# A mixture whose router runs two tiles ahead, with one wide masked product and bias matmuls of 128 rows

## What is computed

```python
h = layernorm(x).reshape(T, 256)                             # T = 2048 tokens
logits = (h @ router_w.T + router_b).reshape(T, O, E)        # O = 256, E = 8
probs = softmax(logits, axis=-1)
w, sel = top_k(probs, 2)
w = w / sum(w, axis=-1, keepdims=True)
c = zeros((T, E)).at[t_idx, sel].add(w)                      # summed over the 256 channels
expert_out = einsum('th,eoh->teo', h, expert_w) + expert_b
x = x + einsum('te,teo->to', c, expert_out)
```

## Time and profile before

| | us |
|---|---|
| median of 3 runs (1390.74 to 1395.88) | 1393.72 |
| the profiled execution | 1396.64 |
| its span | 1394.9 |
| VectorE busy | 1010.1 (72%) |
| TensorE busy | 1107.3 (79%) |
| the mixture, 347 to 718 | 371.0 |

### The profile page before, as it was taken

How to read it: one execution, slowest core, us unless ns; L and a number is a source line. 1 busy time by engine, 2 the same in 40 slices (tenths; PEclk the granted TensorE clock), 3 DMA queues, 4 the chain that set the end, 5 groups by cost and what they waited for, 6 DMA issues and landing times. The chain is left out here.

```text
span 1394.9 us, 19404 instructions
## 1 busy us (share of the span) xinstructions
PE 1107.3 (79%) x6516; PEld 586.0 (42%) x6576; DVE 1010.1 (72%) x1854; ACT 453.5 (33%) x708; POOL 355.1 (25%) x353
## 2 busy tenths in 40 slices
PE   0687878886576979779849788788796789999996
PEld 0243434443333434334313336354372645556564
DVE  7479696874379898999875763946939278777775
ACT  1044343432243242432403331413412034444442
POOL 7024151424224342343430120210203052000000
PEclk9699999998788988899969999999997899999998
DMA  2412112110000100101000000000000010000001
GB/s 90 120 50 60 62 51 72 46 32 4 35 0 0 39 1 0 38 0 38 0 16 1 8 24 1 16 16 0 23 8 15 16 41 6 1 1 0 0 1 61
DMA packets 36263, 34.66 MB, mean 25 GB/s; under 512 B 8024, under 2 KB 32856, under 8 KB 36192
## 3 DMA queue, kind: packets, MB, share of 16 engines
q1 hardware_dynamic: 36192, 33.75, 8.2%
HBM read 27.28 MB, written 6.29 MB: 24 GB/s over the span
## 5 line engine op out<-in xcount | busy, mean ns | idle before, releaser
L926 POOL TENSOR_TENSOR wt<-lg,mid 128x2048 f32<-128x2048 f32 x16 | 75.4, 4710 | 188.4 <-DVE mid L1118 188.4
L750 DVE TENSOR_REDUCE bm<-ps 128x4 f32<-128x512 f32 x160 | 104.5, 671 | 16.6 <-PE ps L547 15.3
L672 ACT ACTIVATE pt<-ps 128x1024 f32<-128x1024 f32 (+1 forms) x96 | 83.0, 881 | 98.6 <-PE ps L593 97.2
L543 PE MATMUL ps<-ks,qs 96*128 96x512 bf16 (+3 forms) x256 | 71.1, 324 | 44.5 <-DVE bm L750 28.1
L1040 ACT ACTIVATE wt<-wt 128x2048 f32<-128x2048 f32 x16 | 30.6, 1914 | 193.9 <-POOL wt L926 193.9
L487 POOL TENSOR_SCALAR_AFFINE_SELECT pt<-pt 128x256 f32<-128x256 f32 (+1 forms) x96 | 46.8, 491 | 154.3 <-ACT pt L672 154.3
L1753 DVE SCALAR_TENSOR_TENSOR g<-g,ps 128x512 f32<-128x512 f32 x64 | 43.9, 686 | 54.2 <-ACT g L1703 54.0
L1497 DVE TENSOR_TENSOR qk_lo<-ps,qk_hi 128x512 bf16<-128x512 f32 x80 | 54.8, 685 | 38.5 <-ACT qk_hi L1399 38.3
L1399 ACT ACTIVATE qk_hi<-ps 128x512 bf16<-128x512 f32 x80 | 47.8, 597 | 102.7 <-PE ps L1290 102.7
L1290 PE MATMUL ps<-xT_hi,wq_hi 128*128 128x512 bf16 x150 | 60.5, 404 | 22.9 <-DVE qk_lo L1497 20.8
L1290 PE MATMUL ps<-wp_hi,oT_hi 128*128 128x256 bf16 x256 | 72.2, 282 | 7.9 <-DVE oT_lo L1489 7.9
(11 more groups left out here) (220 smaller groups left out, 3030.8 us busy)
## 6 DMA issues: line engine op xcount, KB each, us to landing
qs<-scratch_q SPq DMA_DIRECT2D x64, 64.0 KB, 2.6
ks<-scratch_k SPq DMA_DIRECT2D x64, 64.0 KB, 2.6
q_next<-in_w_qkv SPq DMA_DIRECT2D x4, 768.0 KB, 4.5
X<-in_x SPq DMA_DIRECT2D x4, 512.0 KB, 7.0
w_next<-in_router_w SPq DMA_DIRECT2D x4, 512.0 KB, 4.1
w_next<-in_expert_w SPq DMA_DIRECT2D x4, 512.0 KB, 5.0
p_next<-in_w_proj SPq DMA_DIRECT2D x4, 512.0 KB, 5.5
out<-X SPq DMA_DIRECT2D x4, 512.0 KB, 4.9
```

The costliest lines, as they stand in the source:

```text
L543: pe.matmul(ps[:, o + P * i:o + P * (i + w)], qs[0:SHIFT, h, P * j:P * (j + 1)], ks[0:SHIFT, h, P * k0:P * (k0 + w)], start=(i == 0), stop ...
L672: act.activation(pt[kt][:, heads[0]:heads[-1] + 1, :], src, ACT.Exp).then_inc(s_exp, 1)
L750: ins = dve.tensor_reduce(bm[:, 2 * g + i // 5, 4 * (i % 5):4 * (i % 5) + 4], src.rearrange("p (k q) -> p k q", k=4), AX_X, ALU.max)
L926: pool.tensor_tensor(wt[:, :, :], lg[t % 2][:, :, :], over_experts(mid), ALU.subtract).then_inc(s_mid, 1)
```

## The change

The program's other parts stay but for GpSimd's first instructions.

- `tiles` also yields the tile two ahead. TensorE makes `router(n+2)` where it made `router(n+1)`; `router(1)` now stands before the first pass. At t=2 `x_transposed` and `experts(n)` now come before `router(n+2)`. ScalarE makes `logits(n+2)` before `sigmoids(n+1)`, and at t=2 behind `x_parts`.
- `masked`, one product over 128x2048 written into `far`, takes the place of the eight products on VectorE; ScalarE sums its eight parts into `cw` with eight copies (`token_weights`). GpSimd's `from_middle` waits for the product (`kept`), `from_second` for the sums before it overwrites `far`.
- `statistics`, `rstd_ops` and `normalised` of the next batch come one pass earlier, at t=0 and t=1.
- `ones4` and `stage` are 128 rows, all but the first four of them zeros; GpSimd clears both.

```diff
             @block.gpsimd
             def _(pool):
+                pool.memset(glob["stage"][:, :, :], 0.0).then_inc(rows_set, 1)
+                pool.wait_ge(rows_set, 1)
                 for e in range(E):
                     pool.memset(glob["stage"][0:4, 0, D * e:D * (e + 1)], -e * ZERO_STEP).then_inc(rows_set, 1)
-                pool.memset(glob["stage"][0:4, 1, :], 0.0).then_inc(rows_set, 1)
...
         rw_hi, rw_lo, ew_hi, ew_lo = (glob[n] for n in ("rw_hi", "rw_lo", "ew_hi", "ew_lo"))
-        b3 = glob["stage"][0:4, :, :]
+        b3 = glob["stage"]
...
         wp_q = [w[:, :, :].rearrange("p (q h) n -> p q h n", q=B) for w in (glob["wp_hi"], glob["wp_lo"])]
-        ones4 = st.sb("ones4", [4, P], BF16)
+        ones4 = st.sb("ones4", [P, P], BF16)
...
         s_mid, s_far, s_wt, s_cw = st.sem("from_middle"), st.sem("from_second"), st.sem("sigmoids"), st.sem("token_weights")
-        s_c, s_u = st.sem("summed"), st.sem("experts")
+        s_kept, s_c, s_u = st.sem("kept"), st.sem("summed"), st.sem("experts")
         s_abs, s_pert = st.sem("magnitudes"), st.sem("ties_broken")
...
         def tiles(b, last):
+            def later(t):
+                return (b, t) if t < 4 else None if last else (b + 1, t - 4)
             for t in range(4):
-                yield t, 4 * b + t, ((b, t + 1) if t < 3 else None if last else (b + 1, 0))
+                yield t, 4 * b + t, later(t + 1), later(t + 2)
         with nc.Block() as block:
...
                 pool.memset(half[:, :], -0.5).then_inc(const, 1)
-                pool.memset(ones4[:, :], 1.0).then_inc(const, 1)
+                pool.memset(ones4[:, :], 0.0).then_inc(const, 1)
+                pool.wait_ge(const, 2)
+                pool.memset(ones4[0:4, :], 1.0).then_inc(const, 1)
...
                     wait_alone(pool, s_top, TOP * n + TOP, passed_pool)
                     if not isinstance(n, int) or n:
-                        wait_alone(pool, s_cw, E * n, passed_pool)
+                        wait_alone(pool, s_kept, n, passed_pool)
                     pool.tensor_tensor(wt[:, :, :], lg[t % 2][:, :, :], over_experts(mid), ALU.subtract).then_inc(s_mid, 1)
                 rstd_ops(pool, mv, rstd, half, s_mv, s_rstd, 0, passed_pool)
...
                 from_middle(0, 0)
                 def batch(b, first, last):
-                    for t, n, after in tiles(b, last):
-                        if t == 1 and not last:
+                    for t, n, after, _ in tiles(b, last):
+                        if t == 0 and not last:
...
             @block.tensor
             def _(pe):
-                pe.wait_ge(const, 2 + E)
+                pe.wait_ge(const, 3 + E)
                 def products(out, x_hi, x_lo, w_hi, w_lo, cols, bias):
                     pe.matmul(out, ones4[:, :], bias, start=True, stop=False)
...
                 x_transposed(0)
                 router(0, 0, 0)
+                router(0, 1, 1)
                 def batch(b, first, last):
-                    for t, n, after in tiles(b, last):
-                        if after:
-                            router(after[0], n + 1, after[1])
+                    for t, n, _, routed in tiles(b, last):
                         if t == 2 and not last:
                             x_transposed(b + 1)
-                        experts(n, t)
+                            experts(n, t)
+                            router(routed[0], n + 2, routed[1])
+                        else:
+                            if routed:
+                                router(routed[0], n + 2, routed[1])
+                            experts(n, t)
                 all_batches(pe, batch)
...
                 def x_parts(b):
                     reach(act, s_xblo, 4 * b)
+                    reach(act, s_rt, NU * 4 * b)
...
                     act.wait_ge(s_mid, n + 1)
                     act.activation(wt[:, :, :], wt[:, :, :], ACT.Sigmoid, scale=2.0).then_inc(s_wt, 1)
+                def token_weights(n, t):
+                    act.wait_ge(s_kept, n + 1)
+                    for e in range(E):
+                        act.activation(far[:, e, :], far[:, e, :], ACT.Copy, accum_out=cw[t % 2][:, e:e + 1]
+                                       ).then_inc(s_cw, 1)
...
                 sigmoids(0)
+                logits(1, 1)
+                token_weights(0, 0)
                 def batch(b, first, last):
-                    for t, n, after in tiles(b, last):
+                    for t, n, after, routed in tiles(b, last):
                         if after:
                             tile_high(after[0], n + 1, after[1])
-                            logits(n + 1, after[1])
                         if t == 2 and not last:
                             x_parts(b + 1)
+                        if routed:
+                            logits(n + 2, routed[1])
                         if after:
                             sigmoids(n + 1)
+                            token_weights(n + 1, after[1])
                         if t == 0:
                             act.wait_ge(load_next, 32 * b + 32)
...
                 def from_second(n, t):
+                    reach(dve, s_cw, E * n)
                     dve.tensor_tensor(far[:, :, :], lg[t % 2][:, :, :], over_experts(m2), ALU.subtract).then_inc(s_far, 1)
-                def token_weights(n, t):
+                def masked(n):
                     dve.wait_ge(s_far, n + 1)
                     dve.wait_ge(s_wt, n + 1)
-                    for e in range(E):
-                        dve.scalar_tensor_tensor(wt[:, e, :], far[:, e, :], 0.0, wt[:, e, :], ALU.is_ge, ALU.mult,
-                                                 accum_out=cw[t % 2][:, e:e + 1]).then_inc(s_cw, 1)
+                    dve.scalar_tensor_tensor(far[:, :, :], far[:, :, :], 0.0, wt[:, :, :], ALU.is_ge, ALU.mult
+                                             ).then_inc(s_kept, 1)
                 def weigh(b, n, t):
                     c_t = cw[t % 2]
...
                 from_second(0, 0)
-                token_weights(0, 0)
+                masked(0)
                 def batch(b, first, last):
-                    for t, n, after in tiles(b, last):
+                    for t, n, after, _ in tiles(b, last):
+                        if t == 0 and not last:
+                            statistics(b + 1)
                         if t == 1 and not last:
-                            statistics(b + 1)
-                        if t == 2 and not last:
...
                             from_second(n + 1, after[1])
-                            token_weights(n + 1, after[1])
+                            masked(n + 1)
```

## The result

The changed kernel takes 1401.14 us in the median (1400.03 to 1404.95), the kernel before 1393.72 (1390.74 to 1395.88): ratio 1.0058, 95% interval 1.0037 to 1.008. Both medians are of five runs. It is half a per cent slower. The profiled execution took 1400.52 us.

What follows compares the result with a forecast made beforehand. VectorE's order of work was taken to set the pace, with a second chain through ScalarE and TensorE nearly as long. Mixture +5.6, clock +1.3 and starts +0.9 made +7.8 us on 1393.72, so 1401.5; range +2 to +13.

Steps and rivals of the forecast that it cites:

- The rounds: Mixture, from one two_greatest start to the next, t = n mod 4: 19.1, 20.6, 28.9, 20.8 us for t=0 to 3.
- The last batch: Last batch of the mixture: t=0 and t=1 carry no preparation, 18.8 and 20.6 us against 20.75 and 20.5, so -1.9.
- The second chain: ScalarE's and TensorE's work from one wide product's end: sums, |logits|, ties, experts, then weigh, far, product; 17.5 us a round.
- Tail: End of the mixture: sums now stand between the last product and weigh(15), 3.0 - 0.6 + 0.1 = +2.5 us.
- The sums: ScalarE's eight accumulating copies of 128x256: 0.38 us each, 3.0 together, bounds 2.4 and 4.8.
- The bank gaps: TensorE: 0.2 us a bank around the four-row bias matmul, taken to vanish with wider rows; bounds 0 and 0.3.
- The clock: TensorE coming late at 1.2 GHz is no longer hidden by VectorE: +1.3 us for all rounds, bounds 0 and 12.
- The starts: GpSimd's larger clearing of stage costs about 0.65 us, the second clearing of ones4 at the mixture's start 0.25: together +0.9.
- Dear sums: Rival, chance 0.20: ScalarE's sums at 0.5 to 0.6 us each add 10 to 20 us, some 1412.
- The gain that the order suggests: Rival, chance 0.12: the 17.4 us of waits vanish, sums at 0.30 and bank gaps wholly gone, about 1387 us.
- The short stall: Rival, chance 0.10: TensorE is warm or xr_lo earlier, 3 us less in each of three t=2 rounds, 1393.
- No gain from wider matmuls: Rival, chance 0.13: banks stay at 1.7 us, 0.8 us an experts block in eight paced rounds, +6.4, 1408.

Runs made afterwards that it cites:

- a1: The changed kernel measured once more, unaltered, on another chip: 1404.10 us, ratio 1.0078 to the kernel before.
- e6: The changed kernel with TensorE always issuing experts(n) before router(n+2), ScalarE's order kept: 1395.50 us, ratio 1.0009 to the kernel before.
- e11: e7 with the last tile's eight products on VectorE and the clearing of stage moved behind GpSimd's last clearing of qs: 1382.35 us, 0.9903 to before.
- e4: The kernel before with the bias matmuls at 128 rows and nothing else: 1392.25 us, ratio 0.9976 to the kernel before.
- e2: The changed kernel with the bias matmuls at four rows again, the rest kept: 1423.66 us, ratio 1.0201 to the kernel before.
- e7: The changed kernel with the edits of e1 and e6 together: 1383.80 us, ratio 0.9927 to the kernel before; measured again, 0.9897.
- e1: The changed kernel with ScalarE's sigmoids(n+1) ahead of logits(n+2) at t=2 of the first three batches: 1391.47 us, ratio 0.9968 to before.

## Why the prediction came out right

**The forecast time held**, 1401.5 against 1401.14, and the forecast's mechanism is the one that the runs confirm: VectorE waits 6.0 to 6.7 us for the sigmoids once in each of the first three batches, `lg` is waited for at the first tile alone, and `weigh` waits for single experts' banks. That the two times are 0.4 us apart is luck: a1 gave +9.4 us where the first measurement gave +7.4, and terms of 1 to 2 us in the sum were off both ways. By its steps:

- *The rounds.* Forecast 20.8, 19.1, 20.6, 28.9 for t=3, 0, 1, 2; measured 21.2 (first two batches), 19.7, 20.4, 28.2. At t=2 `xr_lo` ended 13.25 us into the round (forecast 13.4) and the four router banks took 7.93 us (taken 8.8, bounds 6.7 to 9.6): only the first is slow.

```profile
536.10 0.61 PE L954 MATMUL ps<-stage,ones 128*128 128x512 bf16 x1 [12.15 <-DVE xr_lo L1105]
...
539.07 0.47 PE L954 MATMUL ps<-stage,ones 128*128 128x512 bf16 x1
...
540.78 0.39 PE L954 MATMUL ps<-stage,ones 128*128 128x512 bf16 x1
```

- *The batches* were summed to +6.3; measured 266.4 against 261.8, +4.6. By position, three rounds each, the forecast was off by -2.0 at t=2, +1.7 at t=0, -0.7 at t=1 and -0.7 at t=3. At t=3 one step was a count: the statistics that open the next batch's first pass were put into three batches, but the third is followed by the last batch, which prepares nothing after it, so its t=3 round is 19.4 and not 21.1.
- *The last batch* was to gain 1.9 us and gained nothing (41.2 against 41.2): its t=0 and t=1 rounds took 19.8 and 21.3 against 18.8 and 20.6. The second chain was taken too short. From the end of one product (481.37) to the end of the next (501.39) it took 20.0 us at t=0 of the second batch, where 17.5 was summed, and 19.8 in the last batch. The forecast's 19.1 at t=0 came near only because VectorE's preparation, 1.7 us with the meetings, was added to a chain that it is not part of: VectorE does it while it would wait anyway. With TensorE's order alone changed (e6) the last batch's rounds are 16.9 and 19.7.
- *Tail*: +2.5 forecast, +3.1 measured (26.8 against 23.7), and e11 took 2.8 of it back. `weigh` waits 3.4 us for the sums, the product gives back 0.6, and the greatest-two chain is 0.3 longer, since `tile_low` now meets it (its operation at 704.59 takes 1.04 us, the same one before 0.69). The product meets GpSimd's last work, as the first of the eight did before (first row):

```profile
708.97 2.23 DVE L1130 SCALAR_TENSOR_TENSOR wt<-far,wt 128x256 f32<-128x256 f32 x1
...
714.98 4.10 DVE L1151 SCALAR_TENSOR_TENSOR far<-far,wt 128x2048 f32<-128x2048 f32 x1
722.45 4.12 DVE L1162 SCALAR_TENSOR_TENSOR X<-ps,cw,X 128x256 f32<-128x256 f32 x8 [3.37 <-ACT far L1056]
```

- *First logits*: -1.0 forecast, -1.7 measured (-0.4 to -0.8 in most of the other traces). *Round before the first*: -0.3 and -0.3.
- *The sums*: taken 0.38 us each; measured 0.40 from start to start, the read-back of each lying beside the next:

```profile
525.73 0.40 ACT L1056 ACTIVATE far<-far 128x256 f32<-128x256 f32 x1
526.04 0.19 ACT L1056 ACTIVATION_READ_ACCUMULATOR far<-far 128x1 f32 x1
526.13 0.40 ACT L1031 ACTIVATE xb_hi<-xf 128x256 bf16<-128x256 f32 x1
```

- *The bank gaps*: taken to vanish. The experts' vanish to the last hundredth (1.51 us is seven steps of 0.215); the router's shrink by 0.27 and leave 0.13. The Trainium skill, "TensorE: Matmul & The Clock Gate", Part 3, says that a weight load overlaps only with matmuls of other row groups. By it e4 and e2 would have shown nothing; they show 4.6 and 19 us, and seven matmuls of 128 rows, weight loads included, run at 0.215 us each, so here the measurement decides against it.
- *The clock* was given 1.3 us for all rounds, and this is the term that was sized too small. In the changed kernel's rows shown with e7, TensorE leaves its wait of 3.44 us (485.56) at a granted clock of 0.50, the mean of 485.5 to 490.4: the eight ties take 2.05 us where unwaited ones take 1.24, and the experts' block behind them 7.8 us in place of the 6.1 of the sum. The nine blocks behind waited ties in the three batches and the round before them take 6.8 to 7.8 us in this trace, those without a wait 6.0, so the slow clock is worth some 12 us in them, an estimate from these rows that lies at the forecast's upper bound. Of the 2.5 us by which the second chain was summed too short at t=0, 1.7 are here. What of it was on the path as a whole, no run shows.
- *The starts*: 0.65 and 0.25 forecast; xn 20.27 us against 19.70, and the wait at the mixture's start 4.90 against 4.67. But attention as a whole ended 3.1 us later than before in this trace, and layer 1's part was 4.9 us shorter, so that the two profiled executions differ by 3.9 us only; in the other traces of kernels with the same start attention ended between 347.3 and 349.9. These are differences between executions, and I leave them unexplained.

The mixture's sum was 5.6, with the clock and the second clearing 7.1; measured +5.7. Against the 5.6, batches and first logits came out 2.4 us below the forecast and last batch and tail 2.5 above it, so the total is closer than its terms.

**The rivals.** *Dear sums* is out at 0.40 us. *The gain that the order suggests* did not come, but its condition was named wrongly: sums of 0.30 and vanished gaps were not what it needed. e7 has the dearer sums and 1383 us, because with experts(n) ahead of router(n+2) the experts no longer stand behind ties that wait for the sums. The prediction had this row of work right ("experts(n) stands behind the ties") and took it as given; that TensorE could take the two the other way round was not asked. *The short stall* did not come; e1 shows what it would have been worth if the order had avoided it. *No gain from wider matmuls* fell with e2 and e4.

## What to carry to other kernels

When work is issued further ahead on an in-order engine, look at what it is placed in front of: the look-ahead removed its waits, and lost more to one place where its input came late and finished work stood behind it. Order each queue by when its reader wants the result; here two such swaps were worth 18 us, more than all that the change itself moved. A saving on the busiest engine is worth nothing while another engine's order makes it wait, so measure parts both alone and together (the same bias edit gave 4.6 and 19 us, the same product cost 0.4 and gave 4.3).

## What the runs showed of the hardware

**A clearing on GpSimd holds VectorE's tensor_scalar of floats.** xn, 128x256 from SBUF to SBUF, took up to 7.09 us beside memsets of 6.95 us and 0.40 us alone; w_lo, with two SBUF inputs, ran its usual 1.76 us at the same time as the first of them, and xT_lo, with PSUM and SBUF, was not held either. The Trainium skill, "SBUF — State Buffer", section "SBUF: two separate sides", agrees: the two engines share a pair of ports under an exclusive lock, which VectorE takes in a two-port mode, or with two SBUF inputs but then only against a GpSimd operation that reads SBUF. Whether xn runs in such a mode, no row shows. What I had not expected is the size: some 16 us at the first scores, as the price of an order.

**A matmul of four rows among matmuls of 128 costs a gap.** 0.2 us for an experts bank and 0.28 for a router bank at 2.4 GHz; at 1.2 GHz a router bank fell from 3.39 us to 2.97. Filling the rows with zeros took the gap away (0.13 us stay at a router bank) at no cost in the matmul itself (0.38 us either way). Why few rows cost it, no run shows.

**ScalarE's accumulating copy** shows as two rows, ACTIVATE 0.40 us and ACTIVATION_READ_ACCUMULATOR 0.19; the next starts 0.40 after it, against 0.30 for a copy without the sum.
